# Lower halves moved to GpSimd, and one row maximum over two neighbouring spans, in a fused attention and FFN kernel

## The reference, cut to what matters

```python
q_pe = _rope(q_pe, cos, sin)
scores = jnp.einsum('bhqd,bhkd->bhqk', qs, ks_) * scale
scores = jnp.where(causal, scores, jnp.finfo(scores.dtype).min)
attn = jax.nn.softmax(scores, axis=-1)
out = jnp.einsum('bhqk,bhkd->bhqd', attn, v)
```

## Time and profile before

| | us |
|---|---|
| median of three runs (lowest, highest) | 1127.04 (1126.23, 1129.42) |
| the profiled execution | 1129.4 |
| its span, first to last instruction | 1127.6 |

### The profile page before, as it was taken

The page is one execution under the profiler, slowest core; times in us unless marked ns, Lnnn a source line. Parts: engine busy times, 40 slices in busy tenths (PEclk is TensorE's granted clock), DMA queues, the critical chain, the costliest instruction groups (busy, mean ns, idle before and its releaser), DMA issues.

```text
span 1127.6 us, 26426 instructions
## 1 busy us (share of the span) xinstructions
PE 975.5 (87%) x10560; PEld 835.3 (74%) x10560; DVE 894.6 (79%) x1383; ACT 734.8 (65%) x1061; POOL 674.3 (60%) x448
## 2 busy tenths in 40 slices
PE   5658898889897989898998889898989898779998
PEld 5536777777786868776877777777778686668887
DVE  5757988897989898889888888888898889772134
ACT  1327786777667867777777777687768686662232
POOL 3655957584849484848485757666675657522332
PEclk7869999999999999999999999999999999899999
DMA  5019999999999999999999998999999899992001
GB/s 164 9 47 173 175 185 156 180 158 180 160 178 159 176 172 178 169 166 171 170 166 167 174 168 165 170 174 163 187 158 182 156 169 199 181 182 75 1 20 57
DMA packets 591979, 170.24 MB, mean 151 GB/s; under 512 B 574064, under 2 KB 585968, under 8 KB 591856
## 3 DMA queue, kind: packets, MB, share of 16 engines
q1 hardware_dynamic: 587376, 167.89, 83.5%
q10 hardware_dynamic: 4480, 0.66, 0.4%
HBM read 15.41 MB, written 2.10 MB: 16 GB/s over the span
## 4 chain that ended last, share of the span: by engine, by line
DVE 19%; PE 19%; issue 7%; SPq 6%; POOL 5%; ACT 3%; DMA 1%; ACTq 0%; POOLq 0%
DVE hl L938 8%; PE s_ps L523 8%; PE s_ps L621 5%; DVE part_max L929 4%; DVE neg_max L927 3%; SPq L459 2%; PE slot_ps L523 2%; SPq L466 2%; POOL hl L1097 2%; PE o_ps L523 2%; POOL pe L1097 1%; DVE acc L901 1%; SPq L453 1%; ACT hl L726 1%; DVE pe_b L886 1%
## 5 line engine op out<-in xcount | busy, mean ns | idle before, releaser
L789 ACT ACTIVATE prob<-s_ps,neg_max 128x1024 f32<-128x1024 f32 (+7 forms) x384 | 318.6, 865 | 209.1 <-DVE neg_max L927 122.2
L1097 POOL TENSOR_TENSOR hl<-prob,hl 128x1024 f16<-128x1024 f32 x128 | 288.3, 2252 | 238.1 <-ACT hl L726 235.5
L929 DVE TENSOR_REDUCE part_max<-s_ps 128x1 f32<-128x1024 f32 (+7 forms) x256 | 244.2, 984 | 80.5 <-PE s_ps L621 66.9
L726 ACT ACTIVATE hl<-prob 128x1024 f16<-128x1024 f32 (+7 forms) x384 | 296.4, 806 | 7.1 <-DMA pT<-hl 5.7
L637 PE MATMUL o_ps<-v,pT 128*128 128x65 f16 x2176 | 232.1, 194 | 65.6 <-DVE o_tiles L950 62.3
L938 DVE TENSOR_TENSOR hl<-prob,hl 128x768 f16<-128x768 f32 (+7 forms) x256 | 279.6, 1132 | 4.5 <-ACT hl L726 2.2
L637 PEld LDWEIGHTS o_ps<-v,pT 128*128 128x128 f16 x2176 | 206.5, 98 | 71.2 <-issue 67.4
L638 PE MATMUL o_ps<-v,pT 128*128 128x64 f16 x2176 | 232.6, 197 | 0.0
L639 PE MATMUL o_ps<-v,pT 128*128 128x65 f16 x2176 | 231.6, 193 | 0.0
L639 PEld LDWEIGHTS o_ps<-v,pT 128*128 128x128 f16 x2176 | 205.9, 100 | 0.0
L638 PEld LDWEIGHTS o_ps<-v,pT 128*128 128x128 f16 x2176 | 205.2, 98 | 0.0
(11 more groups left out here) (183 smaller groups left out, 1994.2 us busy)
## 6 DMA issues: line engine op xcount, KB each, us to landing
q_swap<-q_pe SPq DMA_DIRECT2D x128, 64.0 KB, 2.0
pT<-hl SPq DMA_TRANSPOSE x256, 4.8
wq_sb<-in_L_attn_wq_dram SPq DMA_DIRECT2D x8, 384.0 KB, 4.2
acc<-in_L_attn_x_dram SPq DMA_DIRECT2D x4, 512.0 KB, 6.6
wo_sb<-in_L_attn_wo_dram SPq DMA_DIRECT2D x8, 256.0 KB, 3.2
x_in<-in_L_attn_x_dram SPq DMA_DIRECT2D x1, 2048.0 KB, 8.3
out_dram<-y SPq DMA_DIRECT2D x8, 256.0 KB, 2.1
wkvs<-in_L_attn_wkv_b_dram SPq DMA_DIRECT2D x8, 128.0 KB, 4.1
```

The lines of the kernel that those rows point to most:

```text
L726: return nc.scalar.activation(dst, src, ACT.Copy)
L789: nc.scalar.activation(prob_of(u, m), score_bank(u, m), ACT.Exp, bias=neg_max[:, r:r + 1]).then_inc(exp_done, 1)
L929: nc.vector.tensor_reduce(part_max[:, u % 2, m:m + 1], src, AX.X, ALU.max).then_inc(part_done, 1)
L1097: return lambda: nc.gpsimd.tensor_tensor(dst, a, b, op)
```

## The change

- `lo` halves: of spans 1 and 2, the narrower one (span 2 for k < 8, span 1 for k >= 8; 128, 256, 384 or 512 wide) is computed on POOL, as a step `("rest", u)` after `steps_at(u)`. The DVE keeps the wider one.
- Maximum: one reduction over spans 0 and 1 together (1152 to 2048 wide) takes the place of three.
- Normalising: `o_ps` holds two heads, and `normalise` runs once for two units.
- `q_pe` and `q_swap` have two buffers.
- Rotary sum: POOL adds all 128 rows, and ACT copies head B's 64 rows to `pe_b` (`rope_of_b`).

```diff
-POOL = Steps(POOL_SETUP + [name for u in range(NU) for name in [("low", u)] + steps_at(u)])
+POOL = Steps(POOL_SETUP + [name for u in range(NU) for name in [("low", u)] + steps_at(u) + [("rest", u)]])
+def smaller(u):
+    return 2 if step_of(u) < HALF // 2 else 1
...
             def swap(g, pair):
-                if n >= 1:
-                    before = GROUP_ORDER[(n - 1) % NG], (n - 1) // NG
+                if n >= 2:
+                    before = GROUP_ORDER[(n - 2) % NG], (n - 2) // NG
                     sp.wait_ge(pool_done, POOL.after((f"rope{before[0]}.2", before[1])))
-                    sp.wait_ge(rope_b, n)
...
             def turn_rest(u):
-                sp.wait_ge(lo_dve, 2 * u + 2)
+                sp.wait_ge(lo_dve, u + 1)
+                sp.wait_ge(pool_done, POOL.after(("rest", u)))
...
             def weigh(u, m):
-                if m == 0 and u >= 1:
-                    pe_eng.wait_ge(norm_done, u)
+                if m == 0 and head_of(u) == 0 and u >= 2:
+                    pe_eng.wait_ge(norm_done, u // 2)
-                c0 = (LORA + 1) * (m // 2)
+                c0 = (LORA + 1) * (2 * head_of(u) + m // 2)
...
+            def rope_of_b(g, pair):                      # on ACT
+                act.wait_ge(pool_done, POOL.after((f"rope{g}.2", pair)))
+                copy(pe_b[:, n % 2, :], pe[ROPE:P, n % 2, :]).then_inc(rope_b, 1)
...
             def exponentials(u, m):
                 elif m > 0 and u >= 2:
-                    act.wait_ge(lo_dve, 2 * (u - 2) + 2)
+                    act.wait_ge(lo_dve, u - 1)
+                    act.wait_ge(pool_done, POOL.after(("rest", u - 2)))
...
             def row_max(u, m):
-                nc.vector.tensor_reduce(part_max[:, u % 2, m:m + 1], src, AX.X, ALU.max).then_inc(part_done, 1)
-                if m == 1:
-                    dve.wait_ge(part_done, 2 * u + 2)
-                    nc.vector.tensor_reduce(neg_max[:, r:r + 1], part_max[:, u % 2, :], AX.X, ALU.max, negate=True).then_inc(max_ready, 1)
+                src = score_bank(u, 2) if m else s_ps[:, 0:2 + len(banks(u, 1)), :].rearrange("p b c -> p (b c)")[:, 0:W0 + width(u, 1)]
+                dve.wait_ge(scores_ready, scores_through(u, m or 1))
+                nc.vector.tensor_reduce(neg_max[:, r:r + 1], src, AX.X, ALU.max, negate=True).then_inc(max_ready, 1)
...
             for u in range(-1, NU + LAG + 1):             # on the DVE
-                if u >= LAG + 1:
+                if u >= LAG + 1 and head_of(u - LAG - 1) == 1:
                     normalise(u - LAG - 1)
                 if u + 1 < NU:
                     row_max(u + 1, 0)
-                    row_max(u + 1, 1)
...
-                    prob_low(u, 1)
-                    prob_low(u, 2)
+                    prob_low(u, 3 - smaller(u))
...
             def rope_step(name, pair):
-                    run((name, pair), tt(turned[0:ROPE, :], turned[0:ROPE, :], q_swap[0:ROPE, :], ALU.add))
+                    run((name, pair), tt(turned, turned, q_swap[:, n % 2, :], ALU.add))
...
             for u in range(NU):                           # on POOL
-                prob_low(u)
+                prob_low(u, 0)
                 for name in steps_at(u):
                     step(name)
+                prob_low(u, smaller(u))
```

More of the change, by code:

```diff
@@ L247, in mla_gated_ffn_kernel @@
         sinT = ab("sinT", [P, S])
-        q_pe = ab("q_pe", [P, BANK])
-        q_swap = ab("q_swap", [P, BANK])
+        q_pe = ab("q_pe", [P, 2, BANK])
+        q_swap = ab("q_swap", [P, 2, BANK])
         pe = ab("pe", [P, 2, BANK])
@@ L446, in swap @@
                 n = group_no(g, pair)
-                if n >= 1:
-                    before = GROUP_ORDER[(n - 1) % NG], (n - 1) // NG
+                if n >= 2:
+                    before = GROUP_ORDER[(n - 2) % NG], (n - 2) // NG
                     sp.wait_ge(pool_done, POOL.after((f"rope{before[0]}.2", before[1])))
-                    sp.wait_ge(rope_b, n)
                 for i in range(4):
                     a, b = slice(i * half, (i + 1) * half), slice((i ^ 1) * half, (i ^ 1) * half + half)
-                    sp.dma_start(q_swap[a, :], q_pe[b, :]).then_inc(swapped, 16)
+                    sp.dma_start(q_swap[a, n % 2, :], q_pe[b, n % 2, :]).then_inc(swapped, 16)
             def turn_first(u):
@@ L567, in out_job @@
                 if name.startswith("outT"):
-                    pe_eng.wait_ge(norm_done, pair * PU + 4 * q + 4)
+                    pe_eng.wait_ge(norm_done, (pair * PU + 4 * q + 4) // 2)
                     for j in range(BLK):
@@ L704, in down @@
                 if n == 0:
-                    pe_eng.wait_ge(norm_done, NU)
+                    pe_eng.wait_ge(norm_done, NU // 2)
                 for tp in range(2):
@@ L745, in prep_job @@
                     n = group_no(g, pair)
-                    if n >= 1:
-                        before = GROUP_ORDER[(n - 1) % NG], (n - 1) // NG
-                        act.wait_ge(swapped, 64 * n)
+                    if n >= 2:
+                        before = GROUP_ORDER[(n - 2) % NG], (n - 2) // NG
+                        act.wait_ge(swapped, 64 * (n - 1))
                         act.wait_ge(pool_done, POOL.after((f"rope{before[0]}.0", before[1])))
-                    copy(q_pe[h * ROPE:(h + 1) * ROPE, :], ps[0:ROPE, :])
+                    copy(q_pe[h * ROPE:(h + 1) * ROPE, n % 2, :], ps[0:ROPE, :])
                     if pair > 0:
@@ L780, in job @@
                     prep_job(*name)
+            def rope_of_b(g, pair):
+                n = group_no(g, pair)
+                act.wait_ge(pool_done, POOL.after((f"rope{g}.2", pair)))
+                if n >= 2:
+                    before = GROUP_ORDER[(n - 2) % NG], (n - 2) // NG
+                    act.wait_ge(pool_done, POOL.after((f"B{before[0]}lo", before[1])))
+                copy(pe_b[:, n % 2, :], pe[ROPE:P, n % 2, :]).then_inc(rope_b, 1)
             def exponentials(u, m):
@@ L812, in _ @@
                     prep_job(*name)
+                if name == ("qA0", 0):
+                    rope_of_b(3, 0)
+            rope_of_b(0, 0)
             for u in range(NU + 1):
@@ L821, in _ @@
                 if u < NU:
+                    pair, k = divmod(u, PU)
+                    if k in ROPE_B_OWN:
+                        rope_of_b(ROPE_B_OWN[k], pair)
+                    if k in ROPE_B_NEXT and pair < PAIRS - 1:
+                        rope_of_b(ROPE_B_NEXT[k], pair + 1)
                     prob_high(u, 1)
@@ L877, in query_lo @@
                                         ALU.subtract).then_inc(dve_freed, 1)
[L879 to L886, removed]
             def out_job(name, pair):
@@ L941, in normalise @@
                 pair, k = divmod(u, PU)
-                head = head_of(u)
-                o = o_ps[:, 0:2 * (LORA + 1)].rearrange("p (t c) -> p t c", t=2)
+                n = u // 2
+                o = o_ps[:, 0:4 * (LORA + 1)].rearrange("p (h t c) -> p h t c", h=2, t=2)
+                r = rinv[:, n % 2, :].rearrange("p (h t) -> p h t", h=2)
                 dve.wait_ge(pv_done, scores_through(u))
-                nc.vector.reciprocal(rinv[:, u % 2, :], o[:, :, LORA]).then_inc(recip_done, 1)
-                dve.wait_ge(recip_done, u + 1)
+                nc.vector.reciprocal(r, o[:, :, :, LORA]).then_inc(recip_done, 1)
+                dve.wait_ge(recip_done, n + 1)
                 q, j = divmod(k // 2, 2)
-                if k % 4 == 0 and (q >= 2 or pair > 0):
+                if j == 0 and (q >= 2 or pair > 0):
                     dve.wait_ge(slot_ready, after("ready", (f"outT{(q - 2) % NG}", pair - (q < 2))))
-                nc.vector.tensor_tensor(o_tiles[:, q % 2, 2 * j:2 * j + 2, head * LORA:(head + 1) * LORA],
-                                        o[:, :, 0:LORA], rinv[:, u % 2, :].unsqueeze(2).to_broadcast([P, 2, LORA]), ALU.mult).then_inc(norm_done, 1)
+                nc.vector.tensor_tensor(o_tiles[:, q % 2, 2 * j:2 * j + 2, :].rearrange("p t (h c) -> p h t c", h=2), o[:, :, :, 0:LORA],
+                                        r.unsqueeze(3).to_broadcast([P, 2, 2, LORA]), ALU.mult).then_inc(norm_done, 1)
             def stats(n):
@@ L1030, in _ @@
             values_and_keys(2)
-            rope_of_b(3, 0)
             split_first(3)
@@ L1038, in _ @@
             query_lo(("qB0", 0))
-            rope_of_b(0, 0)
             split_first(0)
@@ L1119, in rope_step @@
                     done = ((queries_split, n - 1),) if 2 <= n < 4 else ()
-                    run((name, pair), tt(turned, q_pe[:], cosT[:, query_cols(g)], ALU.mult), (hi_done, after("hi", (f"qB{g}", pair))),
+                    run((name, pair), tt(turned, q_pe[:, n % 2, :], cosT[:, query_cols(g)], ALU.mult), (hi_done, after("hi", (f"qB{g}", pair))),
                         (tables_loaded[g], 32), *done)
                 elif i == 1:
-                    run((name, pair), tt(q_swap[:], q_swap[:], sinT[:, query_cols(g)], ALU.mult), (swapped, 64 * (n + 1)))
```

(10 more changed lines are left out.)

10 lines of the change are left out of this document (2 added, 8 removed).

## The result

| | before | after |
|---|---|---|
| median of five runs (lowest, highest), us | 1127.36 (1126.23, 1130.85) | 1138.89 (1135.18, 1140.85) |
| ratio, 95% interval | | 1.0084 (1.0059, 1.0108) |
| the profiled execution; its span | 1129.4; 1127.6 | 1139.29; 1137.5 |

The change made the kernel slower by 0.8%, where 1104 us and a gain were forecast. The time lies just inside the range of 1065 to 1140, but on the other side of the likeliest case: it is the second rival's side.

A forecast was written before the change was run, and what follows sets the result against it. POOL was to set the pace in the heavy units. Gains of 2.8 us a pair (19.6 for seven), 2.5 in the last pair and 0.5 in the setup sum to -22.6 us, giving 1104 us, range 1065 to 1140.

The forecast's parts named there:

- the likeliest case: Whole kernel: the unit-by-unit sum through a pair gives 1104 us, own range 1090 to 1118, chance 0.45.
- the second rival: k = 3 to 7 and 11 to 13: POOL as the bound costs more than the DVE did; +20 us, 1147; chance 0.23.
- the walk: Unit-by-unit sum through one pair: 2.8 us a pair shorter, -22.6 us in all.
- e0(4): Start of the first exponential of unit k = 4: foreseen 1.7 us earlier than before, thanks to two buffers.
- e0(9): Start of the first exponential of unit k = 9: foreseen at 610.9 against 610.83 before, the early gain eaten.
- the hold-ups: DVE's wide `lo` and POOL delaying each other: charged to POOL, 2.9 us for k = 3 to 7, 2.1 for 11 to 13.
- units 12 to 15, with the wait for the swap at nothing: End of a pair: POOL sets the pace, units of 7.3, 7.8 and 7.6 us, next pair's first exponential at 658.3 against 661.10.
- one maximum at 0 to 0.1 us a unit: Longer single reduction: 0 to 0.1 us where a TensorE job covers it, taken as 0, plus 0.5 us once a pair.
- cover: k = 1: a TensorE job of 1.4 us ahead of the next scores hides the later exponential; uncovered 0.9 us a unit.
- the third rival: k = 0 to 2 and 8 to 10: longer maximum not covered, 0.5 us each, 3 us a pair; no change, 1126; chance 0.13.

The follow-up runs named there:

- e6: Changed kernel with the DVE writing zeros for the wider `lo` half of spans 1 and 2, reading nothing there: 1104.1 us (0.9769).
- e4: Changed kernel with the four swap DMAs issued ahead of `turn_first` of the same unit instead of behind it: 1110.5 us (0.9831).
- e1: Changed kernel with `rest` undone, both `lo` halves of spans 1 and 2 back on the DVE: 1099.7 us (0.9741).
- e3: Changed kernel with both `rest` and the single maximum undone: 1072.4 us (0.9488).
- e8: Kernel before the change, with only the two buffers for `q_pe` and `q_swap` added: 1095.5 us (0.9698).
- e2: Changed kernel with three reductions again instead of the single maximum, `rest` still on POOL: 1125.0 us (0.9949).
- e7: Changed kernel with `rest` and the single maximum undone (e3), and the swap DMAs ahead of `turn_first`: 1067.4 us (0.9440).
- e9: Changed kernel with `rest` behind the first of a unit's POOL steps instead of behind the last: 1125.5 us (0.9949).
- e12: Kernel before the change, with only the single reduction over spans 0 and 1 added: 1133.4 us (1.0023).
- e11: Kernel before the change, with only one `normalise` for two units added: 1124.0 us (0.9949).

## Why the prediction was wrong

**Right: which queue would be the bound.** POOL busy for 90% of k = 4 to 7, `low` the largest wait of ACT's exponentials, 1.2 us lost by k = 3 (1.3 in the walk), e0(4) 2.1 us earlier than before (1.7), thanks to the buffers. The DVE's busy time came out at 735.6 us (near 700 was foreseen) and POOL's at 781.5 (780). e0(9) at 67.0 after 67.2 in the walk is in part luck: POOL's wait for the swap at k = 4 was 2.5 us where the walk had 1.4, and other terms made up for it.

**Right in kind: the hold-ups; their size is only bounded.** I charged 5.0 us a pair, and e6 got 35 us back in all, 4.4 for each of eight, with other relief in it. They hit the DVE as well, which I had left out: its wide halves took 170 us before and 196 after, most of what its busy time lacks to the 190 us foreseen. A single case is in the trace of before, at the end of the pair that starts at 543.70. POOL works from 652.51 to 654.25:

```profile
652.51 1.74 POOL L1097 TENSOR_TENSOR QA_lo<-pe,QA_hi 64x512 fp32r<-64x512 f32 x1
```

The DVE's `lo` of 128 columns, which takes 0.28 us where POOL is idle, starts at 653.14 and takes 1.26: it ends 0.15 us after POOL's instruction. The rule of the Trainium skill ("SBUF — State Buffer", on the engine side's ports), an exclusive lock between a GpSimd instruction and a DVE one with two SBUF inputs, agrees with this row; the means of 1621 and 1279 ns alone would not tell a lock from slower sharing.

**The step that failed first: units 12 to 15, with the wait for the swap at nothing.** The walk gave k = 12 to 14 7.3, 7.8 and 7.6 us, with no term for the swap that `rope3.1` of k = 11 waits for. POOL waited 3.76 us for it, and k = 12 took 9.47. The queue of SP in the changed kernel:

```profile
618.15 3.02 SPq L462 DMA_TRANSPOSE pT<-hl  x1
621.27 3.26 SPq L470 DMA_TRANSPOSE pT<-hl  x1
624.62 1.95 SPq L462 DMA_TRANSPOSE pT<-hl  x1
626.68 3.14 SPq L470 DMA_TRANSPOSE pT<-hl  x1
629.90 1.95 SPq L462 DMA_TRANSPOSE pT<-hl  x1
631.95 3.74 SPq L456 DMA_DIRECT2D q_swap<-q_pe  x4
635.80 2.73 SPq L470 DMA_TRANSPOSE pT<-hl  x1
```

and POOL's step behind it:

```profile
637.20 1.29 POOL L1098 TENSOR_TENSOR q_swap<-q_swap,sinT 128x512 f32<-128x512 f32 x1 [3.76 <-DMA q_swap<-q_pe]
```

Five transposes, of the units 8 to 10, stand in a row ahead of the swap. The units take 5.8 and 5.9 us each there, SP issues one transpose right behind the other without catching up, and the swap waits its turn. POOL then stands idle for 3.76 us just ahead of its heaviest stretch.

I first put this row down to `rest` of k = 7 and 8 (as in what I expected of e4), which comes late and which `turn_rest` waits for. The other traces say that this is the smaller part. In the mean of pairs 1 to 6 the swap has landed 20.5 us after e0(9) in the changed kernel, and 19.8 in e1, 19.9 in e3 and 19.8 in e8, none of which has `rest`; the row of transposes stands there too. In e2 and e3, which differ by `rest` alone, POOL waits 51.1 and 46.5 us for swaps. So `rest` lengthened the wait by less than 1 us at a time. What it did, as I read e4 beside e7, was to fill POOL's queue, so that a wait which e3 mostly absorbs is paid in full; that the single maximum has no part in this is not shown. The walk had POOL full there and the swap free, and these two did not go together.

e4 prices the swap's place at 28 us. The stretch from k = 12 to the next pair took 31.9 us in the changed kernel (mean of pairs 1 to 6), 29.9 in e4, and 28.9 in the walk. The other half of e4's gain lies ahead of k = 9, where the walk had charged a part of it, so that e4 lands 6 us from my 1104 is no proof of the rest of the sum. e1 is no nearer to the walk in that stretch, with 30.3 us.

**The second: one maximum at 0 to 0.1 us a unit.** I named a TensorE job of 1.4 us as its cover. But that job waits for a PSUM slot that the DVE frees, with an addition that stands behind the longer reduction. The DVE's rows, and TensorE's first matmul of that job, after and before:

```profile
555.24 2.29 DVE L940 TENSOR_REDUCE neg_max<-s_ps 128x1 f32<-128x2048 f32 x1 [2.68 <-PE s_ps L628]
557.45 1.28 DVE L914 TENSOR_TENSOR acc<-slot_ps,acc 128x512 f32<-128x512 f32 x2
```

```profile
558.18 0.53 PE L527 MATMUL slot_ps<-xT_hi,wc_hi 128*128 128x512 f32 x1 [0.98 <-DVE acc L914]
```

```profile
551.02 0.50 PE L523 MATMUL slot_ps<-xT_hi,wc_hi 128*128 128x512 f32 x1
```

Counted from e0(0) the job starts at 8.2 us instead of 7.3, and the next scores at 9.7 instead of 8.8, in each of pairs 1 to 6. The cover moved with the thing it was to cover: k = 0 and 1 take 0.9 us more each, as in e1, e9 and e12 (7.56 us at k = 0 against 6.69), and k = 0 takes 6.7 in e2 and e3, which have three reductions. That is the third rival's mechanism, which I gave 0.13. It costs 14 us here and 27 without `rest`, against 4 in the walk.

**And one comparison never made.** The walk credits the buffers with what they bring and charges the other parts against them, and so the gain of the easy part hid that both headline parts lose: -35 us for the buffers alone, -7 for `normalise`, +14 for `rest` and +3 for the maximum. I priced the whole, and no part by itself. These four add up to -25 us, and the whole change came out at +11.5: the parts are not additive, and a cost that is small alone is not small beside the others.

## What to carry to other kernels

Where a queue is to be filled to the brim, go through everything that it waits for, DMAs and their place in the issuing queue included; here the order of four small DMAs was worth 28 us, on an engine that computes nothing. A cover counts only if its own release doesn't stand behind the instruction it is to cover. Where a change has several parts, price each alone as well: a gain found in one (here two buffers) says nothing for the rest, and undoing `rest` and the single maximum, both meant to unload the DVE, took this kernel from 1138.9 to 1072.4 us.

## What the runs showed that I had not expected

The single maximum costs 2.6 us on the kernel before, 14 beside `rest` and 27 without it; a cost that another bound hides appears when that bound is mended, which is how I read the three. In the first 40 us, before any changed code, profiled executions split between a granted clock near 0.76 and one near 0.54, and the first exponential comes some 3 us later with the lower one (79.28 and 82.28 us); in e11, with 0.50, it came at 88.47. That execution took 1135.8 us against a median of 1124.0, so a single profile's span is no measure of a change below 1%. And the same work on POOL ran in 1139, 1126 or 1220 us depending on its place among the same neighbours.
